# A routed expert layer: the last two tiles' steps reordered, the read-back in token order, one of five sums on GpSimd

## What is computed

```python
x = x + tanh(g_xattn) * cross_attention(ctx, layernorm(x), mask)
# expert layer on layernorm(x):
scores = sigmoid(x_flat @ gate.T + bias)
top_scores, selected = top_k(scores, 2)
top_scores = top_scores / (sum(top_scores) + EPS)
for e in range(9):
    h = silu(x_flat @ w1[e].T) * (x_flat @ w3[e].T)     # hidden width 352
    out = out + cw[:, e:e + 1] * (h @ w2[e].T)
x = x + tanh(g_ffn) * out
```

## Time and profile before

| | us |
|---|---|
| median of three runs | 241.95 |
| the profiled execution | 245.11 |
| its span | 243.3 |
| TensorE busy in the span | 202.1 |
| VectorE busy | 140.0 |
| ScalarE busy | 143.8 |
| GpSimd busy | 124.3 |

### The profile page before, as it was taken

The page is one execution under the profiler, slowest core; times in us unless marked ns, Lnnn a source line. Parts: engine busy times, 40 slices in busy tenths (PEclk is TensorE's granted clock), DMA queues, the critical chain, the costliest instruction groups (busy, mean ns, idle before and its releaser), DMA issues.

```text
span 243.3 us, 5741 instructions
## 1 busy us (share of the span) xinstructions
PE 202.1 (83%) x1530; PEld 159.5 (66%) x1531; DVE 140.0 (58%) x510; ACT 143.8 (59%) x401; POOL 124.3 (51%) x209
## 2 busy tenths in 40 slices
PE   8899896999989999987787970599999999998200
PEld 3577663666656765665565950599999999998100
DVE  0388896687897588987564944134333444442035
ACT  0456969788876876885438520356666666665100
POOL 4228736132335675776684577345555555555400
PEclk9999997999997999999799997589999999999955
DMA  4999999998000100001321131112222211210087
GB/s 125 323 338 323 389 406 372 384 339 300 35 4 12 35 32 12 25 26 45 77 77 45 48 77 44 35 44 65 71 68 53 60 46 45 59 41 26 0 297 220
DMA packets 21146, 30.55 MB, mean 126 GB/s; under 512 B 3313, under 2 KB 14454, under 8 KB 21122
## 3 DMA queue, kind: packets, MB, share of 16 engines
q1 hardware_dynamic: 17282, 25.49, 31.7%
q0 software_dynamic: 2304, 4.24, 5.3%
q10 hardware_dynamic: 1536, 0.54, 0.9%
HBM read 14.72 MB, written 16.05 MB: 126 GB/s over the span
## 4 chain that ended last, share of the span: by engine, by line
PE 59%; DVE 11%; DMA 8%; ACT 6%; issue 6%; another core or an unknown queue 4%; POOL 3%; ACTq 1%; SPq 0%; POOLq 0%; DVEq 0%
PE pt_ps L1160 11%; PE score_ps L1127 6%; PE pt_ps L1169 5%; PE score_ps L1129 5%; PE score_ps L1128 5%; PE score_ps L985 5%; DMA xs<-in_x 4%; PE ps_a L1035 3%; PE pt_ps L1023 3%; DVE xs L943 2%; PE ps_b L1092 2%; PE ps_a L1144 2%; PE ps_b L1090 2%; DMA kheads<-y_rows 2%
## 5 line engine op out<-in xcount | busy, mean ns | idle before, releaser
L557 POOL DMA_INDIRECT y_rows<-probsT,ids x40 | 39.7, 992 | 33.2 <-ACT probsT L445 26.9
L1160 PE MATMUL pt_ps<-w,probsT 128*128 x240 | 35.1, 284 | 11.5 <-ACT probsT L452 11.2
L1160 PEld LDWEIGHTS pt_ps<-w,probsT 128*128 128x128 f32 x240 | 32.3, 197 | 13.1 <-issue 12.5
L377 ACT ACTIVATE probs<-score_ps,less 128x128 f32<-128x128 f32 x128 | 37.6, 408 | 0.4 <-DVE less L748 0.4
L541 POOL DMA_INDIRECT x_rows<-stage,slot x32 | 32.3, 1011 | 8.7 <-issue 8.4
L892 DVE TENSOR_TENSOR xg_low<-ps_a,xg_high 128x128 fp32r<-128x128 f32 x40 | 11.6, 291 | 42.4 <-ACT xg_high L430 41.4
L445 ACT ACTIVATE probsT<-pt_ps,xg 128x128 f32<-128x128 f32 x40 | 14.7, 368 | 35.1 <-PE pt_ps L1160 27.1
L1127 PE MATMUL score_ps<-w_high,xg_low 128*128 x80 | 30.2, 378 | 0.4
L899 DVE TENSOR_TENSOR probs<-probs,score_ps 128x352 f32<-128x352 f32 x40 | 20.8, 521 | 14.6 <-remote 4.5
L1128 PE MATMUL score_ps<-w_low,xg_high 128*128 x80 | 26.5, 331 | 0.0
L1129 PE MATMUL score_ps<-w_high,xg_high 128*128 x80 | 26.4, 331 | 0.0
(11 more groups left out here) (146 smaller groups left out, 416.1 us busy)
## 6 DMA issues: line engine op xcount, KB each, us to landing
x_rows<-pads SPq DMA_DIRECT2D x1, 9945.0 KB, 39.7
w_low<-in_w13T SPq DMA_DIRECT2D x3, 1056.0 KB, 12.4
xg<-x_rows SPq DMA_DIRECT2D x40, 65.0 KB, 1.8
ctx_r<-in_ctxT SPq DMA_DIRECT2D x4, 512.0 KB, 8.5
w<-in_w2T SPq DMA_DIRECT2D x1, 1728.0 KB, 12.4
kheads<-y_rows SPq DMA_DIRECT2D x3, 512.0 KB, 5.1
mask_b<-in_mask SPq DMA_DIRECT2D x4, 256.0 KB, 9.2
xs<-in_x SPq DMA_DIRECT2D x3, 256.0 KB, 8.1
```

The lines of the kernel that those rows point to most:

```text
L377: last = nc.scalar.activation(probs[:, r % 2, h, :], score_ps[:, r % 2, h, :], ACT.Exp, bias=less[:, r % 2, h:h + 1])
L557: pool.indirect_dma_start(y_rows[:, :], bass.IndirectOffsetOnAxis(ap=ids[:, r:r + 1], axis=0), yt[:, r, :], None, bounds_check=last_row, o ...
L1160: last = nc.tensor.matmul(bank[5][:, 0:D], hidT[:, q3, c, :], w2[:, bass.ds(e3, 1), c, :].rearrange("p o d -> p (o d)"), start=(c == 0), s ...
```

## The change

1. **Token order.** Labels are now `(b * 128 + t) * 2 + c`, so that `y_rows` lies in token order, b outermost. The read-back gives partition p the 16 tokens from 16p on.
2. **x2 takes a detour.** `xs` has to be in that order too. SP stores all of `xs` to `out` (1 MB) ahead of the load of tile 8, once the last x2 is there, and loads it back into `xs` after the last tile load. The read-back of the parts waits for it (`x2_back`). The stores at the end write 2 KB (or 1 KB) in a piece for each partition.
3. **The drain.** The hidden values of the last tile (39) are turned in step 40 into `bank[0]`, right after those of tile 38; DVE and not ACT copies them; their w2 product goes to `bank[1]` behind that of tile 38. GpSimd copies the labels of tiles 38 and 39 together, ahead of the scatter of 38.
4. **The sum.** GpSimd adds part 1; DVE adds 0, 2, 3 and 4. Stores are issued in the order 0, 2, 1, 3, 4.

```diff
+POOL_PART, DVE_PARTS = 1, (0, 2, 3, 4)
@@ sync
+            out_tok = out.rearrange("b t d -> (b t) d").rearrange("(p n) d -> p n d", p=P)
             for n in range(len(EARLY)):
+                if n == 1:
+                    sp.wait_ge(x2_done, NB * 2 - 1)
+                    sp.dma_start(out.rearrange("b t d -> t b d"), xs[:]).then_inc(x2_stored, 16)
                 sp.wait_ge(rows_known, n + 1)
...
+            sp.wait_ge(x2_stored, 16)
+            sp.wait_ge(ln2, NB)
+            sp.dma_start(xs[:], out_tok).then_inc(x2_back, 16)
             for r in range(TR):
                 sp.wait_ge(st_y[r], (NT // TR) * 16)
-            y_tok = y_rows.rearrange("(t b c) d -> t b c d", t=P, c=2)
+            y_tok = y_rows.rearrange("(p n c) d -> p n c d", p=P, c=2)
+            sp.wait_ge(x2_back, 16)
             for g, here in enumerate(PARTS):
                 sp.dma_start(ys[:, here, :, :], y_tok[:, here, :, :]).then_inc(ld_y[g], 16)
-            for g, here in enumerate(PARTS):
-                sp.wait_ge(y_added, 2 * g + 2)
-                sp.dma_start(out[here].rearrange("b t d -> t b d"), xs[:, here, :]).then_inc(st_out, 16)
+            for g in (*DVE_PARTS[:2], POOL_PART, *DVE_PARTS[2:]):
+                if g == POOL_PART:
+                    sp.wait_ge(added_pool, 2)
+                else:
+                    sp.wait_ge(y_added, 2 * DVE_PARTS.index(g) + 2)
+                sp.dma_start(out_tok[:, PARTS[g], :], xs[:, PARTS[g], :]).then_inc(st_out, 16)
@@ gpsimd
-                pool.wait_ge(ids_cast, k + 1)
-                nc.gpsimd.tensor_tensor(ids[:, r:r + 1], ids_in[:, r:r + 1], zero[:], ALU.add).then_inc(ids_copied, 1)
-                pool.wait_ge(ids_copied, k + 1)
+                for t in {NT - 2: (k, k + 1), NT - 1: ()}.get(k, (k,)):
+                    at = t % TR
+                    pool.wait_ge(ids_cast, t + 1)
+                    nc.gpsimd.tensor_tensor(ids[:, at:at + 1], ids_in[:, at:at + 1], zero[:], ALU.add).then_inc(ids_copied, 1)
+                    pool.wait_ge(ids_copied, t + 1)
...
+            pool.wait_ge(x2_back, 16)
+            pool.wait_ge(ld_y[POOL_PART], 16)
+            for c in range(2):
+                nc.gpsimd.tensor_tensor(xs[:, here, :], xs[:, here, :], ys[:, here, c, :], ALU.add).then_inc(added_pool, 1)
+                pool.wait_ge(added_pool, c + 1)
@@ vector
+                if is_last(k - 1):
+                    cast_ids(NT - 2, (NT - 2) % TR, (NT - 2) // TR)
+                    cast_ids(NT - 1, (NT - 1) % TR, (NT - 1) // TR)
+                    dve.wait_ge(hid_turned, NT)
+                    dve.wait_ge(y_mm, NT - 2)
+                    nc.vector.tensor_copy(hidT[:, (NT - 1) % 2, :, :], bank[0][:, 0:NC * P].rearrange("p (c t) -> p c t", c=NC)).then_inc(last_copied, 1)
@@ tensor
+                if is_last(k - 1):
+                    pe.wait_ge(hid_done, NT)
+                    for c, c0 in enumerate(CH):
+                        last = nc.tensor.transpose(bank[0][:, c * P:(c + 1) * P], hid[:, (NT - 1) % 2, c0:c0 + P], ident)
+                    last.then_inc(hid_turned, 1)
```

More of the change, by code:

```diff
@@ L230, in has, with is_last @@
             return not isinstance(k, int) or 0 <= k - lag < NT
+        def is_last(t):
+            return isinstance(t, int) and t == NT - 1
         @block.sync
@@ L444, in tile @@
                         act.wait_ge(st_y[place], turn * 16)
-                    nc.scalar.activation(yt[:, place, :], bank[5][:, 0:D], ACT.Copy, scale=xg[:, place, C_WEIGHT:C_WEIGHT + 1]).then_inc(y_done, 1)
-                if has(k, 2):
+                    nc.scalar.activation(yt[:, place, :], bank[1 if is_last(t) else 5][:, 0:D], ACT.Copy, scale=xg[:, place, C_WEIGHT:C_WEIGHT + 1]).then_inc(y_done, 1)
+                if has(k, 2) and not is_last(k - 2):
                     t, q = k - 2, r % 2
@@ L572, in _ @@
                         scatter(NG - 1, p)
+            here = PARTS[POOL_PART]
+            pool.wait_ge(x2_back, 16)
[3 more added lines that the diff above has]
+                pool.wait_ge(added_pool, c + 1)
         @block.vector
@@ L727, in weigh @@
                                                ALU.mult, ALU.mult).then_inc(weighed, 1)
[L728 removed]
+                nc.vector.tensor_scalar(stage[:, g % 2, :, :, C_ID], part["first_ids"].rearrange("p (c b) -> p c b", c=2), 2.0 * UN * P * g, None, ALU.add)
                 assert route_links["weigh"] == LINKS["weigh"]
@@ L885, in _, with cast_ids @@
             unturn(NB - 1, 1)
+            def cast_ids(t, place, turn):
+                dve.wait_ge(ld_tile[place], turn * 16 + 16)
+                if not isinstance(t, int) or t >= TR:
+                    dve.wait_ge(st_y[place], turn * 16)
+                nc.vector.tensor_copy(ids_in[:, place:place + 1], xg[:, place, C_ID:C_ID + 1]).then_inc(ids_cast, 1)
             def tile(k, r, i):
@@ L937, in _ @@
             tile_turns(dve, tile, between)
-            for g, here in enumerate(PARTS):
+            for n, g in enumerate(DVE_PARTS):
+                here = PARTS[g]
+                if g == 0:
+                    dve.wait_ge(x2_back, 16)
                 dve.wait_ge(ld_y[g], 16)
@@ L1155, in tile @@
                     e3 = expert(r - 3)
-                    pe.wait_ge(hid_copied, t3 + 1)
-                    if not isinstance(t3, int) or t3 >= 1:
-                        pe.wait_ge(y_done, t3)
+                    into = bank[5]
+                    if is_last(t3):
+                        pe.wait_ge(last_copied, 1)
+                        into = bank[1]
+                    else:
+                        pe.wait_ge(hid_copied, t3 + 1)
+                        if not isinstance(t3, int) or t3 >= 1:
+                            pe.wait_ge(y_done, t3)
                     for c in range(NC):
-                        last = nc.tensor.matmul(bank[5][:, 0:D], hidT[:, q3, c, :], w2[:, bass.ds(e3, 1), c, :].rearrange("p o d -> p (o d)"),
+                        last = nc.tensor.matmul(into[:, 0:D], hidT[:, q3, c, :], w2[:, bass.ds(e3, 1), c, :].rearrange("p o d -> p (o d)"),
                                                 start=(c == 0), stop=(c == NC - 1))
                     last.then_inc(y_mm, 1)
-                if has(k, 2):
+                if has(k, 2) and not is_last(k - 2):
                     t2, q2 = k - 2, r % 2
```

13 lines of the change are left out of this document (6 added, 7 removed).

## The result

The changed kernel took 247.45 us (median of four runs, 246.34 to 248.63), the kernel before 242.78 (four runs, 241.64 to 245.51). The ratio is 1.0174, with a 95% interval from 1.0118 to 1.0230. So the change made this kernel slower by 1.2 to 2.3%. I had forecast 242.5, and at most 245.4.

What follows compares the result with a forecast made beforehand. TensorE was taken to bound the tiles, before an ending of some 18 us without matmuls. 245.11 - 0.62 (drain) + 1.15 (blocking) = 245.6 profiled, 242.5 us median; own range 241.9 to 243.4, 8 in 10 240.7 to 245.4.

Steps and rivals of the forecast that it cites:

- The drain: Last tiles: the scatter of 39 starts 0.30 behind that of 38, a gain of 0.62 us, bounds 0.3 and 0.65.
- Rival 2: At the last scatter: the drain gives nothing, something other than the label copy holds scatter 39; 243.1 us, chance 0.15.
- The sum: Final additions: GpSimd's second addition blocks DVE's part 2, costing +1.15 us, bounds 0 and 1.3.
- Rival 1: Final additions: GpSimd and DVE do not block each other, or GpSimd finishes before part 2 lands; 241.3 us, chance 0.2.
- Stores: Final stores after the additions: reordering and longer pieces cost 0, bounds -0.2 and +0.8 us.
- Store of x2 ... Cost 0: Ahead of tile 8's load: the 1 MB store, 3.3 us of all DMA engines, costs 0, or up to 3.3.
- rival 3: Tiles: the 1 MB store lengthens TensorE's standstill between 143 and 155 us by up to 3.3, to 245.8; chance 0.12.

Runs made afterwards that it cites:

- set 2: Four kernels beside the kernel before on one chip, testing GpSimd's adding against its late end; the changed kernel 1.0058, with one GpSimd addition 1.0004.
- set 1 without GpSimd: The changed kernel with DVE adding all five parts and GpSimd none, x2 stored early: 230.41 us, 1.0029 to the kernel before.
- set 2 changed: The changed kernel again, unedited, on another chip: 246.29 us, 1.0058 to the kernel before.
- one addition: The changed kernel with GpSimd doing one of part 1's two additions and DVE the other, behind part 2: 244.43 us, 1.0004 to the kernel before.
- set 4 changed: The changed kernel again, unedited, beside three variants on one chip: 232.64 us, 1.0110 to the kernel before.
- store only: The kernel before with only the 1 MB store of x2 added, at the place where the change has it: 230.65 us, 1.0033.
- set 3 early store: The changed kernel without GpSimd in the sum, x2 stored early, register load in its place: 229.78 us, 1.0019 to the kernel before.
- set 4 filled: The changed kernel with twelve and not four filling matmuls ahead of the last x2 row's transpose: 232.35 us, 1.0086 to the kernel before.
- set 2 late store: The changed kernel without GpSimd in the sum and with x2 stored behind the last tile load: 243.53 us, 0.9947 to the kernel before.
- touch: The kernel before with the new drain and a tiny GpSimd memset waiting for the last part of the read-back: 245.37 us, 1.0012.
- set 3 late store: The changed kernel without GpSimd in the sum, x2 stored behind the last tile load, on another chip: 228.99 us, 0.9975 to the kernel before.
- set 1's late store: The changed kernel, GpSimd still in the sum, with x2 stored behind the last tile load: 231.15 us, 1.0048 to the kernel before.

## Why the prediction was wrong, and where it was right

**The drain: right.** The step said that the scatter of 39 would start 0.30 behind that of 38, for a gain of 0.62. It does (228.86 and 230.16, less 0.99), and the ending is 0.6 shorter with the drain alone. Rival 2 falls.

**The sum: right in its mechanism, a little too high.** The prediction said that GpSimd's second addition would run into DVE's part 2, "DVE was blocked and not slowed", and took +1.15. It measured 1.65 - 0.70 = +0.95 on the addition, +0.85 on the whole sum (7.05 for 6.2). The first addition of DVE ended 0.56 after GpSimd's, so most of an addition's own length still lay behind the lock. The prediction had also said that with DVE first the end is the same within 0.15: DVE's end was then 0.26 earlier, but GpSimd's 0.5 later, and GpSimd's end counts. Rival 1 falls as the likely case, but set 2 shows that its condition was well put: with one GpSimd addition, done before part 2, DVE keeps 0.70. The Trainium skill, page "SBUF — State Buffer", section "Who interferes with whom", has the shared port pair as an exclusive lock for a whole instruction; the trace agrees with 1.65 against 0.70.

**"Stores": the step that failed in the ending.** It read "I take 0, bounds -0.2 and +0.8". The stores themselves are as I had them (the last one lands in 2.0, before 1.8). What was missing is a term: the change puts work at the end of GpSimd's program, and with it the closing drain, which had been hidden by 243.1 - 235.4 = 7.7 us of cover. After the change it is +0.85 (246.55 against 245.7). The trace before would have shown it: GpSimd's last instruction ends at 229.46 and SP's program at 243.1, and the closing rows have 5.9 us behind the former. I had asked when each engine's additions end, and not when each engine's program ends.

**"Store of x2 ... Cost 0": the step that failed in the middle.** It was priced as a matter of bandwidth and of SP's queue, and rival 3 looked for its victim at the standstill after 143 us. The victim was 2 us behind the store: TensorE's register load, 0.31 long before and 1.14 after, with 0.13 and 0.91 of idle time. So rival 3, the store holding up the tiles, is what happened, but at another place, and its term of "up to 3.3" is in fact 0.5 to 0.8 for the gap itself. The Trainium skill, page "DMA: Bandwidth & Descriptors", section "Latency and other measured facts", states a floor of about 600 ns for a `tensor_load`. The traces do not bear that out: this load takes 0.31 in the kernel before, half of it, and only beside the store does it take more.

**The sum of the profiled execution.** Drain -0.6, blocking +0.85, GpSimd's late end with the slightly later store +0.95, gives +1.2 in the ending. The middle has +2.3: 0.3 already there at the router's product, 0.8 for the gap, 1.3 for the tile at half clock, of which 0.65 are given back by tile 5, and 0.6 behind it. Together 3.5, the difference of the spans. Of the middle only the gap is shown to come from the change.

**What stays open.** Why the clock fell at tile 3. In the profiles with the early store and the load in its place, tile 3 took 3.8 to 4.3 us in five (the changed kernel, set 1 without GpSimd, set 2 changed and one addition, set 4 changed) and 2.5 in three (store only; set 3 early store; set 4 filled). But it also took 3.3 to 4.0 in three profiles without the early store (set 2 late store and touch, set 3 late store), and 2.5 in the kernel before, in both of the drain alone and in set 1's late store. With the load moved it was 2.4 in all three. What goes with it better is the idle time ahead of the last x2 rows: in all five profiles in which TensorE idled 2.0 to 2.1 us there, with the early store or without it, tile 3 ran at half clock. Three more did so after 1.11, 0.70 and none, and none of the four with 1.4 did. So the gap may tip the clock over, and something else can as well; one profile per kernel does not settle it. Open is also the size: the first comparison has 1.2 to 2.3%, sets 2 and 4 have 0.6% and 1.1% for the same kernel. The shown costs, 0.8 for the gap and 1.2 in the ending, make 2.0 us, which lies between the 1.5 of set 2 and the 3.1 of set 4 (by the medians); that the first comparison has 4.7 is not explained by what was shown.

## What to carry to other kernels

Before giving the last work of a program to an idle engine, look up when that engine's own closing instructions end, not only its work: an engine that finishes early covers some 6 us of closing time that cost nothing until it is given something to do at the end. A second adder helps only in the time in which the first one has data to add and does not share its port, so compare landings first. A large transfer put into a "quiet" place should be checked against every small load there, register loads included, which the timeline does not show and the view of their line does; where one is needed soon after, load the register early.

## What the runs showed of the hardware that I had not expected

- **GpSimd's closing drain.** Counted from the end of GpSimd's last instruction it ends 6.1 us later after two additions (240.44 to 246.55), 6.0 after a memset (239.20 to 245.20), 6.0 after one addition (237.81 to 243.77) and 5.9 after the last scatter before the change (229.46 to 235.38). Whether the earlier indirect DMAs are what it waits for was not tried.
- **Register loads and DMA.** A register load out of SBUF took 0.31 us and cost TensorE 0.1 with the DMA engines quiet; with a 1 MB store running it took 0.99 to 1.14 and cost 0.56 to 0.91.
- **Two adders take turns.** Where additions of GpSimd and DVE overlap, the one that comes second is the longer one: 1.65 and not 0.70 for DVE, 1.77 and 1.82 and not 1.26 for GpSimd.
- **Chips differ by a standstill.** Between tiles 9 and 10 the transposes are 13.5 us apart in the kernel before on the first chip (its wait is the earlier trace rows), 13.2 after, and 12.5 to 13.3 in set 2; in sets 1, 3 and 4 they are 2.5 apart. That is 11 of the 14 us between 244 and 230 for one and the same kernel. What releases it has no row, and the change does not move it. Its cause stays open.
- **Filling matmuls bought nothing.** With twelve of them the clock was 1.00 over tile 3, as it also was in profiles without them, and the median was that of the kernel without them within the interval.
